# Self-attention's weighted sums with the values as weights: four column groups, sixteen heads to a group of four products, and the sums turned back by four transposes

## The reference

```python
x = x + _L0_attn_ref(_layernorm(x), L0_attn_Wq, L0_attn_Wkv, L0_attn_Wo)

def _L0_attn_ref(hidden_states, Wq, Wkv, Wo):
    q = (hidden_states @ Wq).reshape(b, s, NUM_HEADS, HEAD_DIM)      # 32 heads of 16
    kv = hidden_states @ Wkv
    k, v = (kv[..., :HEAD_DIM], kv[..., HEAD_DIM:])
    scores = jnp.einsum('bqhd,bkd->bhqk', q, k) * scale
    scores = jnp.where(causal[None, None], scores + bias[None], -jnp.inf)
    attn = jax.nn.softmax(scores, axis=-1)
    out = jnp.einsum('bhqk,bkd->bqhd', attn, v).reshape(b, s, h)
    return out @ Wo
```

## Time and profile before

| | |
|---|---|
| median of 3 runs | 1013.65 us (1013.39 to 1013.73) |
| the profiled execution | 1013.56 us, its span 1011.7 us |
| PE | busy 983.9 us, 97% of the span, granted clock 0.992 of 2.4 GHz |
| DVE | busy 592.7 us, 59% |
| ACT | busy 429.5 us, 42% |
| POOL | busy 381.9 us, 38% |
| self-attention | from 0 to about 232 us of the span |

### The profile page before, as it was taken

How to read it: one execution, slowest core, us unless ns; L and a number is a source line. 1 busy time by engine, 2 the same in 40 slices (tenths; PEclk the granted TensorE clock), 3 DMA queues, 4 the chain that set the end, 5 groups by cost and what they waited for, 6 DMA issues and landing times. The chain is left out here.

```text
span 1011.7 us, 15673 instructions
## 1 busy us (share of the span) xinstructions
PE 983.9 (97%) x5096; PEld 806.0 (80%) x5096; DVE 592.7 (59%) x973; ACT 429.5 (42%) x1239; POOL 381.9 (38%) x375
## 2 busy tenths in 40 slices
PE   5999999989999999999999999999999989999998
PEld 3777777877888888888888888888888768888787
DVE  3766666636776676666766657667666873343100
ACT  2777777751532533533533433533432543333100
POOL 6422222253652642642642633634523422222200
PEclk8999999989999999999999999999999999999999
DMA  6000000211120210210210210200200112222001
GB/s 202 13 11 11 11 10 10 63 52 52 41 61 5 63 43 0 73 31 0 73 31 0 73 31 0 81 23 13 80 0 1 33 32 70 65 71 67 11 32 42
DMA packets 49954, 39.98 MB, mean 40 GB/s; under 512 B 4128, under 2 KB 40096, under 8 KB 49920
## 3 DMA queue, kind: packets, MB, share of 16 engines
q1 hardware_dynamic: 49536, 38.48, 12.9%
q0 software_dynamic: 384, 1.05, 0.4%
HBM read 37.43 MB, written 2.10 MB: 39 GB/s over the span
## 5 line engine op out<-in xcount | busy, mean ns | idle before, releaser
L617 PE MATMUL bank<-cross_wo_hl,cross_outT_hl 128*128 128x512 f32 x768 | 191.7, 398 | 1.0 <-POOL cross_wo_hl L611 0.6
L617 PE MATMUL bank<-hsT_hl,cross_wqkv_hl 128*128 128x512 f32 x768 | 188.2, 394 | 0.0
L617 PEld LDWEIGHTS bank<-cross_wo_hl,cross_outT_hl 128*128 128x128 f32 x768 | 143.1, 188 | 35.5 <-POOL cross_wo_hl L611 1.6
L617 PEld LDWEIGHTS bank<-hsT_hl,cross_wqkv_hl 128*128 128x128 f32 x768 | 141.9, 188 | 29.3
L932 ACT ACTIVATE cross_scores<-cross_scores,cross_negmax 128x128 f32<-128x128 f32 x256 | 99.8, 391 | 127.2 <-DVE cross_negmax L870 127.2
L792 POOL TENSOR_TENSOR cross_qT<-rotated,rotated_other_half 128x512 f32<-128x512 f32 x64 | 82.8, 1293 | 161.9 <-DVE rotated_other_half L834 161.9
L617 PE MATMUL bank<-hsT_hl,ff_gate_upT_hl 128*128 128x512 f32 (+1 forms) x528 | 120.4, 390 | 2.7 <-DVE ff_gate_upT_hl L1134 2.7
L617 PEld LDWEIGHTS bank<-hsT_hl,ff_gate_upT_hl 128*128 128x128 f32 (+1 forms) x528 | 97.7, 185 | 25.0 <-DVE ff_gate_upT_hl L1134 3.1
L942 ACT CAST cross_outT_hl<-bank 128x512 fp32r<-128x512 f32 x64 | 37.1, 580 | 143.4 <-PE bank L617 142.5
L832 DVE TENSOR_TENSOR rotated<-bank,cosT 128x512 f32<-128x512 f32 x80 | 55.2, 691 | 71.3 <-PE bank L617 71.1
L617 PE MATMUL bank<-ctxT_hl,cross_wqkv_hl 128*128 128x512 f32 x384 | 94.3, 394 | 1.1 <-PEq L74 1.1
(11 more groups left out here) (115 smaller groups left out, 1534.9 us busy)
## 6 DMA issues: line engine op xcount, KB each, us to landing
staged_rows<-in_wq SPq DMA_DIRECT2D x32, 256.0 KB, 2.9
staged_rows<-in_wo SPq DMA_DIRECT2D x32, 256.0 KB, 2.7
staged_rows<-in_wg SPq DMA_DIRECT2D x10, 256.0 KB, 2.9
staged_rows<-in_wu SPq DMA_DIRECT2D x10, 256.0 KB, 2.9
staged_rows<-in_wd SPq DMA_DIRECT2D x10, 256.0 KB, 2.8
ctx_tok<-in_ctx SPq DMA_DIRECT2D x8, 256.0 KB, 2.6
staged_rows<-in_wk SPq DMA_DIRECT2D x8, 256.0 KB, 3.1
staged_rows<-in_wv SPq DMA_DIRECT2D x8, 256.0 KB, 3.1
```

What stands on the lines that cost most here:

```text
L617: i = nc.tensor.matmul(out, stationary[:, a], moving[:, b], start=(first and k == 0), stop=(last and k == 2))
```

## The change

The two factors of the weighted sums change places. The values with the ones (`v_ones`, 32 columns, of which the seventeenth to the last are ones) are now the weights, and the turned probabilities are streamed, 512 columns of four heads at a time. A product with 32 weight columns fills a quarter of the array's columns and writes 32 partitions, so the four quads of a half go to four column groups, partitions 0, 32, 64 and 96 of one bank `OB`. `PT` gets four buffers to hold half a sequence. The sums then stand turned (features on the partitions), so ACT copies the bank into `outT`, four transposes turn it back into another bank, `NB`, and `normalise` reads that one. The values lie in what will later be `cosT`, `outT` in what will be `sinT`; both are written with their own contents in turn 8, as before.

```diff
-    SC, TB, OB, G = ps[0:2], ps[2:4], ps[4:6], ps[6:8]
+    SC, TB, OB, NB, G = ps[0:2], ps[2:4], ps[4], ps[5], ps[6:8]
...
-        v = sb("self_v_and_ones", [P, SEQS, HD1 + 1])
+        v = m["cosT"][:, 0:SEQS * HD1].rearrange("p (b d) -> p b d", b=SEQS)
+        v_ones = m["cosT"][:, DM:DM + 2 * HD1]
...
-        PT = sb("self_probsT", [P, 2, QUAD, P])
+        PT = sb("self_probsT", [P, HALF, QUAD * P])
...
+        outT = m["sinT"][:].rearrange("p (i k) -> p i k", i=2)
...
                 for s in range(STEPS):
                     n = STEPS * b + s
-                    if s == 3 and since(b, 1):
+                    if s == 0 and since(b, 1):
+                        normalise(b - 1, 0)
+                    if s == 4 and since(b, 1):
                         normalise(b - 1, 1)
...
-                    if s == 7 and scores:
-                        normalise(b, 0)
...
+            def copy_probsT(b, s):
+                if not since(b, 1) and s < 2 or since(b, SEQS) and s >= 2:
+                    return
+                act.wait_ge(sem["probs_transposed1"], STEPS * b + s - 1)
+                if since(b, 1) or s >= 6:
+                    act.wait_ge(sem["pv1"], 2 * b + (s - 2) // HALF)
+                nc.scalar.copy(PT[:, (s - 2) % HALF], TB[s % 2][:]).then_inc(sem["probsT1"], 1)
+
+            def copy_outT(b, i):
+                k = 2 * b + i
+                act.wait_ge(sem["pv1"], k + 1)
+                if since(b, 1):
+                    act.wait_ge(sem["outT_turned1"], k - 1)
+                nc.scalar.copy(outT[:, i], OB[:]).then_inc(sem["outT1"], 1)
...
                         e.then_inc(sem["exp1"], 1)
+                    if s % HALF == 2:
+                        copy_probsT(b, s)
+                    if (s == 2 and back) or (s == 6 and scores):
+                        copy_outT(b - 1 if s == 2 else b, 1 if s == 2 else 0)
...
+            def weighted_sums(b, i):
+
+                k = 2 * b + i
+                pe.wait_ge(sem["probsT1"], HALF * (k + 1))
+                pe.wait_ge(sem["v_ready"], b + 1)
+                if i == 1 or since(b, 1):
+                    pe.wait_ge(sem["outT1"], k)
+                for c in range(HALF):
+                    e = nc.tensor.matmul(OB[32 * c:32 * c + 32, :], v_ones, PT[:, c, :], start=True, stop=True)
+                e.then_inc(sem["pv1"], 1)
+
+            def turn_outT(b, i):
+                k = 2 * b + i
+                pe.wait_ge(sem["outT1"], k + 1)
+                if i == 1 or since(b, 1):
+                    pe.wait_ge(sem["attn"], k)
+                for h in range(QUAD):
+                    e = nc.tensor.transpose(NB[:, h * P:(h + 1) * P], outT[:, i, h * P:(h + 1) * P], ident[:])
+                e.then_inc(sem["outT_turned1"], 1)
...
-                        for j in range(QUAD):
-                            c = (QUAD * (r % HALF) + j) * (HD1 + 1)
-                            i = nc.tensor.matmul(OB[r // HALF][:, c:c + HD1 + 1], PT[:, r % 2, j, :], v[:, bass.ds(owner, 1), :].rearrange("p b d -> p (b d)"),
-                                                 start=True, stop=True)
-                        i.then_inc(sem["pv1"], 1)
+                    if (s == 2 and back) or (s == 6 and scores):
+                        weighted_sums(b - 1 if s == 2 else b, 1 if s == 2 else 0)
+                    if (s == 3 and back) or (s == 7 and scores):
+                        turn_outT(b - 1 if s == 3 else b, 1 if s == 3 else 0)
```

More of the change, by code:

```diff
@@ L263, in normalise @@
                     dve.wait_ge(sem["attn_transposed"], b)
-                nc.vector.tensor_tensor(attn[:].rearrange("p (i h d) -> p i h d", i=2, h=16)[:, i], o[:, :, 0:HD1],
-                                        rsum[:, 16 * i:16 * i + 16].unsqueeze(2).to_broadcast([P, 16, HD1]),
+                nc.vector.tensor_tensor(attn[:].rearrange("p (i c h d) -> p i h c d", i=2, c=HALF, h=QUAD)[:, i], o[:, :, :, 0:HD1],
+                                        r.unsqueeze(3).to_broadcast([P, QUAD, HALF, HD1]),
                                         ALU.mult).then_inc(sem["attn"], 1)
@@ L348, in copy_kv @@
                 act.wait_ge(sem["kv1"], c + 1)
-                if first:
-                    act.wait_ge(sem["ones_ready"], 1)
-                else:
+                if not first:
                     act.wait_ge(sem["kexp"], c)
@@ L360, in copy_qT, with copy_v @@
                 nc.scalar.copy(qT[:, HALF * half:HALF * (half + 1), :], G[1][:].rearrange("p (s k) -> p s k", s=HALF)).then_inc(sem["qT"], 1)
+            def copy_v(b):
+                if since(b, 1):
+                    act.wait_ge(sem["pv1"], 2 * b)
+                else:
+                    act.wait_ge(sem["ones_ready"], 1)
+                nc.scalar.copy(v_ones[:, 0:HD1].unsqueeze(1), v[:, bass.ds(b, 1), :]).then_inc(sem["v_ready"], 1)
+            def copy_probsT(b, s):
[8 more added lines that the diff above has]
+                act.wait_ge(sem["pv1"], k + 1)
+                if since(b, 1):
+                    act.wait_ge(sem["outT_turned1"], k - 1)
+                nc.scalar.copy(outT[:, i], OB[:]).then_inc(sem["outT1"], 1)
             copy_xnT(0, first=True)
@@ L378, in body @@
                         copy_qT(b, 1)
[L379 to L384, removed]
+                    if s % HALF != 2:
+                        copy_probsT(b, s)
+                    if s == 3 and scores:
+                        copy_v(b)
                     if s == 7 and not since(b, 1):
```

12 lines of the change are left out of this document (7 added, 5 removed).

## The result

The changed kernel takes **1015.92 us**, the median of 8 runs (1014.7 to 1017.48), against 1013.69 us of 8 runs of before (1013.39 to 1014.02): a ratio of 1.0023 with an interval of 1.0012 to 1.0034. It is slower by 2.2 us, where 12.1 us were forecast; the time lies inside the range and far from the number. The difference is small: the kernel before, run again beside the experiments, took between 1011.84 and 1018.10 us. The profiled execution took 1015.98 us, its span is 1014.2 us, 2.5 us longer than that of before.

What follows compares the result with a forecast made beforehand. PE was taken to bound the kernel, a turn lasting as long as its list. Turns 2 to 6 lose 6.7 us, the end 3.5, the borders 1.9: 12.1 on 1013.56 gives 1025.7 us, range 1012 to 1044.

Steps and rivals of the forecast that it cites:

- T: Joint PE time of a set's four wide products: 2.13 us, bounds 0.86 and 3.4; prediction wrong outside 1.3 to 3.
- the borders: Array shape changes into and out of each set of wide products: 0.16 us per set, 1.9 in turns 1 to 6.
- Turns 2 to 6: The five loop turns laid out like turn 4: each 1.34 us longer, 6.7 in all.
- the end: Chain from the stage's last copy of a quad to the `attn` transposes: 7.0 us instead of 3.5, 3.5 lost.
- turn 7: Last turn, held to be set by a transfer that POOL's chain releases, a fixed time after its start: change 0.
- The bound at the other end, 0.86: Lowest cost in us of a set's four wide products, if all four stream at the same time.
- all at once: Rival: all four wide products stream together, T 0.86, a turn 25.3 us, 0.26 shorter, kernel 1012.3 us; chance 0.15.
- step 4: Fifth of a turn's eight steps: to start 11.96 us after the turn's first scores, 11.83 before; 11.6 under "all at once".
- steps 4 and 5: Moved `normalise` adds 0.62 us on DVE to the chain to `k_low`: 6.11 us instead of 5.91, 0.20 lost.
- step 6: Seventh step of a turn, 1.00 + 2.13 (T) + 1.70 = 4.83 us on PE instead of 3.50: loss 1.33.
- step 7: Last step of a turn, set by the copy of the queries: 4.0 us instead of 4.32, gain 0.32.
- Turns 0 and 1: First two turns, both put at 0, between 1.5 us gained and 1.5 lost.
- PE's sum: Rival: PE's saved work decides; turns 1 to 6 win 1.36 us each, the end loses 3.5, kernel 1009; chance 0.10.

Runs made afterwards that it cites:

- Experiments 1 to 3: Changed kernel with its four wide products on four source lines, 1015.51 us; all on one column group, 1044.62 us; alternating between two column groups, 1022.09 us.
- Experiments 4, 7 and 8: 4: changed kernel, `normalise(b - 1, 1)` between `q_low` and `k_low`, 1012.97 us; 7: experiment 6 plus queries' copy ahead of step 7's exponentials, 1004.26 us; 8: see experiment 8.
- experiment 6: Changed kernel with `normalise(b - 1, 1)` between `q_low` and `k_low` and turn 7's `ctx_low` behind the last quad's maximum: 1007.77 us.
- experiment 5: Changed kernel with only turn 7's `ctx_low` moved one step later, behind the bias and maximum of the last quad: 1010.9 us.
- experiment 8: Experiment 6 with the queries' copy ahead of step 7's exponentials, plus half 1's `turn_outT` one step later, ahead of the key product: 1002.4 us.

## Why the prediction was wrong in its size, and right in its direction by luck

**T was mis-sized, and with it the turn: this is the step that failed.** "If PE starts its passes in the order of the list", with the second pass of a product ahead of the next product's first, was a guess, which no row of before could bear out; T came out as 2.13 us, and 0.16 for the borders. Measured are 1.00 with all borders in it, below the 1.3 at which the prediction calls itself wrong. Experiments 1 to 3 show what happened instead: the first passes of all four groups run side by side, then the second ones, and only passes of one group follow each other. Who put them in that order, PE or the list, is open. Turns 2 to 6 were to get 6.7 us longer and five sixths of the borders' 1.9, 8.3 in all, and came out 0.05 shorter all together: that is 8.3 of the 9.6 us by which the sum of 12.1 exceeds the 2.45 of the two spans. The rest nearly cancels: the end 2.3, turn 1 1.8, turn 0 with the start 1.1 and the cross stage's head 0.2 less than laid out, and some 4 more in turn 7. The bound at the other end, 0.86, was the right neighbour; I chose against it since a product has two passes, and the passes of one group are just what sets 0.86.

**The direction was luck.** With T = 1.00 the forecast would have been near the rival's 1012.3, no change. The changed kernel is slower because turn 7 with the end took 5.29 us more, up to 4.87 of it by a collision that no part of the prediction has; all the other stretches together took 2.84 us less.

**The layout of the turn held.** With T = 1.00 put into it, step 4 starts at 11.6 where the sums' copy holds PE (measured 125.75 - 114.41 = 11.34), steps 4 and 5 take 6.11 (measured 6.12), step 6 takes 1.00 + 1.00 + 1.70 = 3.70 (measured 3.80), step 7 4.0 (4.33): 25.4, and 25.59 were measured. The waits stand where they were laid out: on `x1` 0.49 (0.5 forecast), on `hs_low` 0.77 (0.8), and at `attn` PE goes on 5.71 us after step 4's start (5.72). The 1.9 us that the prediction wanted to see as waiting for `k_low` at `attn` do not fit the prediction's own layout, which splits it into 0.8 at the key product and the rest, 1.0, at `attn`; 0.84 were measured there. Experiments 4, 7 and 8 cut or remove three of the five waits, and the turn gets shorter each time. So "all at once" was the case that came, its turn 0.26 us shorter by the forecast and 0.03 longer as measured.

**Step 7 had no cover to give.** The 4.0 for step 7 counted 0.4 us between the end of the queries' copy and the next scores as cover. After the change the scores start 0.39 behind the copy (139.61 and 140.00), just as before (142.29 and 142.67). Here are that copy in the kernel after, and the one ahead of turn 7 with the scores that follow it.

```profile
139.05 0.56 ACT L361 CAST self_qT_high_above_low<-bank 128x512 fp32r<-128x512 f32 x1
...
190.24 0.56 ACT L361 CAST self_qT_high_above_low<-bank 128x512 fp32r<-128x512 f32 x1
190.85 0.73 PE L543 MATMUL bank<-self_k_by_head_hl,self_qT_high_above_low 128*128 128x512 f32 x2
```

Ahead of turn 7, which is written out, the gap is 0.05 us, and so it is ahead of turns 1 and 2. Only the turns of the loop have 0.37 to 0.50; there PE has a few short instructions on registers between the wait and the scores, which the views do not list. So step 7 was already set by the copy and what PE does behind it, and 4.33 for 4.32 is no gain. Of the 0.32 expected there nothing came.

**Turn 7 was not "0".** I took it as set by a transfer that POOL releases, and put it at nothing; what came was a collision of two engines, which the new times bring together. It costs up to 4.87 us (experiment 6 against the changed kernel), and moving `ctx_low` alone shows it to be the cause (experiment 5). The end itself, forecast 3.5 us longer, is 1.2 longer: from the last copy of a quad (its row is below, 220.86 + 0.58 = 221.44) to the `attn` transposes 4.71, 3.50 before, since T is smaller there too, 1.93 at the lower clock for the 4.27 laid out.

```profile
220.86 0.58 ACT L376 COPY self_probsT<-bank 128x512 f32<-128x512 f32 x1 [0.74 <-PE bank L552]
```

**Turns 0 and 1** were put at 0 within 1.5 us: turn 1 gained 1.51, at the bound, and turn 0 with the start 1.07. Their waits were not tried one by one, and the clock of turn 0 was not the same before and after.

**PE's sum** did not decide; it begins to where covers are given back. In experiment 8 PE is busy for 22.19 of 23.74 us, 1.5 us of waiting a turn where the changed kernel has 2.9.

## What to carry to other kernels

Small work that stands in every step also covers a wait in every step. When it is gathered into lumps, list the waits that it covered before counting the time that PE saves: here 2.7 us a turn were saved, 2.8 us of waits came up, and only moving four small pieces of work turned most of the saving into time (23.74 us a turn for 25.56). When a resource is new to the kernel and its bounds lie far apart (0.86 and 3.4), what lies between them is a guess, and the range should be read from the ends. And when earlier stages get shorter, look at what two engines then do at the same moment: a 0.69 us instruction became one of 7.18.

## What the runs showed of the hardware that was not expected

- **Column groups run beside each other, and both passes of a product need not follow at once.** Four float32 products with 32 weight columns each, 512 columns streamed, cost 1.00 us on four groups, 1.85 on two, 3.56 on one. The Trainium skill, "TensorE: Matmul & The Clock Gate", Part 3, has products on different column groups run at the same time, and the trace agrees; it also has matmuls start strictly in order, and here the second pass of the first product starts 0.43 us behind the first pass of the last (119.04 and 118.61). Whether that breaks the rule no run here shows, since the order in PE's list is not in the trace.
- **A DVE instruction can be held for a whole row of POOL instructions.** `ctx_low`, two inputs from SBUF, lasts 0.69 us alone and 7.18, 7.82 and 5.05 us beside POOL's six subtractions (the changed kernel, experiments 4 and 5), and it ends 0.55 to 0.57 us behind the last of them each time. The Trainium skill, "SBUF — State Buffer", section "Who interferes with whom", says that a DVE instruction with two SBUF inputs contends with a POOL instruction that reads SBUF, and that contention on the ports they share is an exclusive lock; the trace agrees and shows more: it did not get in between the six.
- **The granted clock differs between executions of one kernel.** Of experiment 6's six runs the three near 1005 us have a mean granted clock of 0.995, the three near 1011 one of 0.986; only one of the latter has a trace. At the end of the stage four transposes take 1.09 to 1.11 us in the changed kernel and in experiment 6, the lower level, and 0.63 to 0.66 in experiment 5, the upper one.
